# A four-layer gated block on one core: scores in quads of heads, gate weights spread on TensorE, gathers for depool and heads, another load queue, filler transposes, another order

## The reference

```python
x = x + tanh(g_xattn[0]) * L0_xattn(ctx, layernorm(x), mask, ...)   # cross attention, 8 heads of 16
x = x + tanh(g_ffn[0])   * L0_ffn(layernorm(x), ...)                # 4 of 16 attention heads of 64, picked per batch
x = x + tanh(g_xattn[1]) * L1_xattn(layernorm(x), ctx, lens, ...)   # depool of a scan over ctx, plus a projection
x = x + tanh(g_ffn[1])   * L1_ffn(layernorm(x), ...)                # 8 experts, top 2 per token, plus a shared one
```

## Time and profile before

| | before |
|---|---|
| runs | 243.16 us median of 3 (242.94 to 246.14) |
| profiled execution, first to last instruction | 242.8 us |
| PE busy | 211.0 us (87%), 1154 instructions |
| DVE busy | 151.1 us (62%), 464 instructions |
| ACT busy | 104.6 us (43%), 283 instructions |
| POOL busy | 54.0 us (22%), 95 instructions |
| mean granted TensorE clock | 0.895 |

### The profile page before, as it was taken

How to read it: one execution, slowest core, us unless ns; L and a number is a source line. 1 busy time by engine, 2 the same in 40 slices (tenths; PEclk the granted TensorE clock), 3 DMA queues, 4 the chain that set the end, 5 groups by cost and what they waited for, 6 DMA issues and landing times.

```text
span 242.8 us, 3827 instructions
## 1 busy us (share of the span) xinstructions
PE 211.0 (87%) x1154; PEld 152.9 (63%) x1154; DVE 151.1 (62%) x464; ACT 104.6 (43%) x283; POOL 54.0 (22%) x95
## 2 busy tenths in 40 slices
...
GB/s 198 293 82 195 79 230 327 1 65 54 33 44 72 65 45 25 3 1 0 1 37 33 0 0 37 34 0 3 22 0 0 4 1 22 0 3 0 0 0 43
DMA packets 17139, 12.45 MB, mean 51 GB/s; under 512 B 9024, under 2 KB 16416, under 8 KB 16992
## 3 DMA queue, kind: packets, MB, share of 16 engines
...
...
## 4 chain that ended last, share of the span: by engine, by line
PE 52%; DVE 1%; issue 1%; ACT 0%; ACTq 0%; DVEq 0%
PE dve_bank L655 7%; PE act_bank L647 7%; PE act_bank L648 6%; PE act_bank L650 4%; PE act_bank L594 3%; PE dve_bank L584 3%; PE act_bank L576 3%; PE dve_bank L640 2%; PE dve_bank L615 2%; PE dve_bank L669 2%; PE act_bank L660 2%; PE act_bank L449 2%; PE act_bank L561 1%; PE act_bank L512 1%; PE dve_bank L660 1%; PE dve_bank L612 1%
## 5 line engine op out<-in xcount | busy, mean ns | idle before, releaser
L769 ACT ACTIVATE hx<-act_bank,we 128x256 f32<-128x256 f32 x32 | 15.2, 475 | 36.1 <-PE act_bank L650 36.1
L1065 POOL TENSOR_TENSOR ctok<-ctok,cT 128x256 f32<-128x256 f32 x28 | 20.4, 729 | 44.6 <-DVE cT L994 43.5
L913 DVE TENSOR_REDUCE mx<-dve_bank 128x2 f32<-128x512 f32 x32 | 20.7, 686 | 10.4 <-PE dve_bank L496 10.3
L725 ACT ACTIVATE pT<-act_bank 128x512 f32<-128x512 f32 x32 | 17.6, 596 | 15.1 <-PE act_bank L512 14.9
L994 DVE SCALAR_TENSOR_TENSOR cT<-dve_bank,we,hx 128x256 f32<-128x256 f32 x32 | 15.0, 482 | 10.8 <-PE dve_bank L655 10.8
L1021 POOL TENSOR_SCALAR veps<-mv 128x2 f32<-128x2 f32 x16 | 3.1, 191 | 83.9 <-DVE mv L849 83.7
L647 PE MATMUL act_bank<-xw,we 128*128 128x256 f32 x64 | 20.3, 399 | 0.0
L655 PE MATMUL dve_bank<-hx,we 128*128 128x256 f32 x64 | 19.5, 404 | 0.2 <-ACT hx L770 0.2
L987 DVE TENSOR_TENSOR xw<-xnT,dve_bank 128x512 f32<-128x512 f32 x16 | 10.9, 684 | 13.3 <-PE dve_bank L640 13.3
L648 PE MATMUL act_bank<-xw,we 128*128 128x256 f32 x64 | 19.0, 379 | 0.0
L496 PE MATMUL dve_bank<-kstack,qstack 49*128 49x256 f32 x64 | 14.9, 368 | 4.5 <-DMA qstack<-parts 4.5
...
## 6 DMA issues: line engine op xcount, KB each, us to landing
we<-pack_e ACTq DMA_DIRECT2D x1, 1932.0 KB, 11.2
...
```

The lines of the kernel that those rows point to most:

```text
L725: act.activation(pT1[:, i].rearrange("p c t -> p (c t)"), bank[:], ACT.Exp, scale=HD1 ** -0.5).then_inc(act_done, 1)
L769: act.activation(hx[:, k % EXPERT_BUFS, 0, :], bank[:, 0:T], ACT.Silu, bias=X("b1")[:, i:i + 1])
L913: dve.tensor_reduce(mx[:, b, :, i], bank[:].rearrange("p (t s) -> p t s", t=TT), AX.X, ALU.max).then_inc(dve_done, 1)
L1065: ins = pool.tensor_tensor(yT[:, b % 2, :], yT[:, b % 2, :], prod[:, k % EXPERT_BUFS, :], ALU.add)
```

## The change

The program is rewritten in many places and its steps are put in another order. Part by part:

- **Scores.** A step of `s1` or `st1` now does four heads: each head stands in its own 32 partitions, with 16 rows of features, a row of the mask and a row of the maximum (17 or 18 contraction rows), as plain F32, and the four are issued to the four row groups in turn. There are two such steps a batch (`SETS`) for eight before. The projections give this layout themselves (twice the columns), so `parts` and all of `restack` are gone. The maxima come back through a transpose and a DVE addition into `qs` (`max1`), not a DMA. The mask is loaded as three rows and spread by a matmul (`masks`).
- **Heads.** `s2` takes two heads a step, issued to partitions 0 to 63 and 64 to 127 in turn. The bias of a head is one more column of its weights, and of the four loads SP issues two and POOL two, as indirect DMAs. `scale2` leaves DVE's 16 reciprocals and moves the 32 multiplications of 128x256 to POOL. Every second `pt2` is emptied by ACT instead of DVE.
- **Depool.** `plan_c` gives row numbers at once for all batches. DVE scales `dp`, SP stores it in DRAM, POOL gathers its rows with two indirect DMAs a batch (`gather`), and `base` adds them. The matmuls with `pick` are gone.
- **Experts.** `wide` does all four pairs in one step with F32 matmuls of 16 rows in four row groups. `b3` is a bias in ACT's copy, so L650 is gone; what it leaves out for the unchosen experts is taken from a small table (`ktab`) with one more matmul for each half of `y4`.
- **Loads.** Nearly all loads are issued from SP, at the start, in one sequence; ACT issues `pack_a`, the mask selectors and the second batch's `x`.
- **Fillers.** At 26 steps PE does 2 to 40 transposes of the identity into a bank that is taken next (180 in all), and 16 matmuls before the first step.
- **Rings.** Four banks each, for three and five.

```diff
-ACT_RING, DVE_RING = 3, 5
+ACT_RING, DVE_RING = 4, 4
...
+        "s1": (0, 4), "max1": (0, 1), "st1": (4, 0), "pv1": (1, 0), "heads1": (0, 1), "o1": (1, 0), "y1": (0, 1),
+        "route": (0, 1), "qkv2": (3, 0), "s2": (2, 0), "pv2": (1, 0), "y2": (0, 1),
...
+KEEP_WARM = {
+    ("norm", 1, 0): 8,
+    ("s1", 0, 1): 7,
...
+    ("norm", 1, 3): 40,
...
+            def keep_warm(step, count):
...
+                if n >= ring:
+                    pe.wait_ge(done, n - ring + 1)
+                for k in range(count):
+                    pe.transpose(bank[:, 0:P], ident, ident)
...
+                    banks = [take_dve(nd + j) for j in range(QUADS)]
+                    for t in range(TT):
+                        for j in range(QUADS):
+                            lo, hi = 32 * j, 32 * j + ROW_MAX
+                            mm = pe.matmul(banks[j][:, t * T:(t + 1) * T], qs[lo:hi, b % 2, i, t * P:(t + 1) * P],
+                                           ks[lo:hi, b % 2, i, :], start=True, stop=True, tile_position=(lo, 0))
...
-                    pe.matmul(bank[:, T:2 * T], X("w3")[:, i * D:(i + 1) * D], xe, start=True, stop=False
-                              ).then_inc(up_read, 1)
-                    pe.matmul(bank[:, T:2 * T], b3s[:, i, :], gT[:, b, :], start=False, stop=True
-                              ).then_inc(act_full, 1)
+                    pe.matmul(bank[:, T:2 * T], X("w3")[:, i * D:(i + 1) * D], xe, start=True, stop=True
+                              ).then_inc(act_full, 1)
...
-                    act.copy(hx[:, k % EXPERT_BUFS, 1, :], bank[:, T:2 * T]).then_inc(act_done, 1)
+                    act.activation(hx[:, k % EXPERT_BUFS, 1, :], bank[:, T:2 * T], ACT.Identity,
+                                   bias=X("b3")[:, i:i + 1]).then_inc(act_done, 1)
...
+                elif what == "scale2":
+                    pool.wait_ge(rec2_done, NA * b + i + 1)
+                    for t in range(TT):
+                        ins = pool.tensor_scalar(p2[:, b % 2, i, t, :], p2[:, b % 2, i, t, :], rec2[:, b, i, t:t + 1], 1.0,
+                                                 ALU.mult, ALU.mult)
+                    ins.then_inc(p2_scaled, 1)
...
+                elif what == "gather":
...
+                    pool.wait_ge(dp_out[b], 16)
+                    for t in range(TT):
+                        m = b * TT + t
+                        pool.indirect_dma_start(out=dpg[:, m, :], out_offset=None, in_=dp_rows[b],
+                                                in_offset=bass.IndirectOffsetOnAxis(ap=plug[:, m:m + 1], axis=0)
+                                                ).then_inc(dp_in[b], 16)
```

More of the change, by code:

```diff
@@ L68 @@
-ORDER = """
[L69 to L73, removed]
@@ new lines @@
+ORDER = """
+stat:0.0 masks:0.0 norm:0.0 stat:1.0 kv:0.0 q:0.0 masks:1.0 norm:1.0 s1:0.0 s1:0.1 max1:0.0 q:1.0 max1:0.1
+u:0.0 st1:0.0 kv:1.0 stat:2.0 st1:0.1 s1:1.0 pv1:0.0 pv1:0.1 gates:0.0 masks:2.0 heads1:0.0 s1:1.1 base:0.0
+o1:0.0 y1:0.0 max1:1.0 stat:0.1 ktab:0.0 masks:3.0 norm:0.1 norm:2.0 stat:3.0 max1:1.1 route:0.0 st1:1.0 q:2.0
+kv:2.0 st1:1.1 plan_a:0.0 s1:2.0 qkv2:0.0 pv1:1.0 s2:0.0 s2:0.1 scale2:0.0 depool:0.0 plan_b:0.0 scale2:0.1
+depool:1.0 max1:2.0 scale2:0.2 pt2:0.0 pv1:1.1 scale2:0.3 pt2:0.1 plan_c:0.0 pt2:0.2 heads1:1.0 pv2:0.0
@@ new lines @@
+base:0.1 pt2:0.3 gather:0.0 s1:2.1 pv2:0.1 o1:1.0 y2:0.0 st1:2.0 consts:0.0 base:0.2 base:1.0 stat:0.2
+max1:2.1 y1:1.0 stat:1.1 pv1:2.0 norm:0.2 norm:3.0 norm:1.1 y3:0.0 route:1.0 st1:2.1 q:3.0 gather:1.0 kv:3.0
+pv1:2.1 s1:3.0 qkv2:1.0 stat:0.3 depool:2.0 base:1.1 s2:1.0 heads1:2.0 scale2:1.0 s2:1.1 scale2:1.1 o1:2.0
+norm:0.3 scale2:1.2 pt2:1.0 pt2:1.1 scale2:1.3 max1:3.0 gather:2.0 pt2:1.2 gate:0.0 pt2:1.3 pv2:1.0 s1:3.1
+pv2:1.1 gate_t:0.0 y2:1.0 base:1.2 st1:3.0 max1:3.1 base:2.0 y1:2.0 st1:3.1 stat:2.1 stat:1.2 norm:2.1 pv1:3.0
@@ new lines @@
+norm:1.2 route:2.0 pv1:3.1 wide:0.0 shared:0.0 up:0.0 up:0.1 y3:1.0 stat:1.3 qkv2:2.0 up:0.2 s2:2.0 down:0.0
+heads1:3.0 down:0.1 s2:2.1 scale2:2.0 scale2:2.1 scale2:2.2 norm:1.3 scale2:2.3 pt2:2.0 pt2:2.1 pt2:2.2 o1:3.0
+pt2:2.3 gate:1.0 pv2:2.0 pv2:2.1 base:2.1 up:0.3 down:0.2 y2:2.0 up:0.4 base:2.2 base:3.0 stat:2.2 y1:3.0
+stat:3.1 down:0.3 shared:1.0 up:0.5 up:0.6 norm:3.1 norm:2.2 down:0.4 gate_t:1.0 route:3.0 up:0.7 wide:1.0
+down:0.5 up:1.0 down:0.6 y3:2.0 up:1.1 stat:2.3 down:0.7 qkv2:3.0 up:1.2 norm:2.3 s2:3.0 down:1.0 s2:3.1
@@ new lines @@
+y4:0.0 scale2:3.0 scale2:3.1 depool:3.0 down:1.1 scale2:3.2 gate:2.0 gather:3.0 down:1.2 pt2:3.0 shared:2.0
+scale2:3.3 up:1.3 pt2:3.1 up:1.4 pt2:3.2 up:1.5 down:1.3 base:3.1 gate_t:2.0 up:1.6 pt2:3.3 down:1.4 up:1.7
+wide:2.0 pv2:3.0 pv2:3.1 down:1.5 down:1.6 y2:3.0 stat:3.2 down:1.7 up:2.0 up:2.1 base:3.2 up:2.2 norm:3.2
+down:2.0 down:2.1 y3:3.0 up:2.3 stat:3.3 down:2.2 up:2.4 up:2.5 norm:3.3 down:2.3 gate:3.0 down:2.4 down:2.5
+y4:1.0 shared:3.0 gate_t:3.0 up:2.6 up:2.7 wide:3.0 up:3.0 down:2.6 up:3.1 down:2.7 up:3.2 down:3.0 down:3.1
@@ L121 @@
 NORMS = list(NORM_AT)
[L122 removed]
 XN_BUFS = 4
 EXPERT_BUFS = 3
+XW_BUFS = 4
+WARM_UP = 16
 def expert(k):
```

885 lines of the change are left out of this document (503 added, 382 removed), and 2 rows, old and new, of the table ROW_MAX.

## The result

The changed kernel takes 217.95 us (median of four executions, 214.15 to 219.52) against 243.18 before, a ratio of 0.884 with a 95% interval of 0.872 to 0.897: 11.6% faster. Each ratio here is taken from the executions in the faster of two states (here 214.15 and 216.92 us) and the kernel before run beside them, so it is not the quotient of the medians. The forecast was 202 us in a range of 186 to 224. So sign and range held, and the point lies 16 us too low. The profiled execution took 214.15 us, with a span of 212.4; against it the sum of 201.6 is 10.8 too low. The other executions differ from the profiled one in the granted clock (0.992 there, 0.966 to 0.984 in the others), and experiment 6 finds where.

What follows compares the result with a forecast made beforehand. Batch 0's chain with waits, partly at half clock, was taken to bound the time before the first wide matmul, PE's work the time behind it: 102.8 + 98.8 = 201.6, forecast 202 us, range 186 to 224.

Steps and rivals of the forecast that it cites:

- link 5: Batch 0's y2 to the first wide matmul: set by DVE's 30 us plus 3.5 for waits, 33.5 us.
- stage B: From batch 0's first wide matmul to the end: PE's work is the time, 112.3 - 18.2 + 4.7 = 98.8 us.
- rival (d): Fillers don't hold the clock before the first wide matmul, which stays at 1.2 GHz: slower, total 260 us; chance 0.05.
- Links 1 and 3: Batch 0: start to first scores, 20.6 to 14.0 us; y1 to first qkv2, 22.1 to 12.5 us.
- rival (e): Gathers fail their purpose, heads arrive no earlier, +5 in batch 0 and +5 behind: 212 us; 0.26 with (b), (c).
- Link 2: Batch 0's first scores to y1: less waiting for maxima and rs, cheaper pv1, kv of batch 1 added; 31.2 to 21.7 us.
- Link 4: Batch 0's first qkv2 to y2: POOL's scale2 at 2.6 us a head paces the softmax; 26.2 to 21.1 us.
- (b): Score matmuls on four row groups overlap only two at a time: +12, 214 us; chance 0.26 together with (c), (e).
- (c): POOL becomes the bound through scale2 and gathers, stalling down's three buffers: 217 us; chance 0.26 together with (b), (e).
- (a): POOL's scaling is cheap, 0.8 us a head, and waits overlap: 190 us; chance 0.22.
- stage A: Everything before the first wide matmul: batch 0's chain through three layers with waits and half clock; 130.5 to 102.8 us.

Runs made afterwards that it cites:

- experiment 6: Changed kernel with the ktab step moved later: 220.84 us; with ktab in place and 13 filler transposes added in and behind it: 216.1 us.
- experiment 3: Changed kernel with the scaling of the second softmax on DVE instead of POOL: 217.75 us.
- experiment 1: Changed kernel without its 180 filler transposes: 224.31 us; with only the 105 before the first wide matmul: 219.67; with only the 75 behind it: 221.91.
- experiment 5: Changed kernel with an added matmul of eight rows by 256 columns before the second matmul of every up, 32 in all: 244.5 us.
- Experiments 3 and 4: 3: changed kernel, softmax scaling on DVE, 217.75 us. 4: batch 0's first wide and shared moved earlier, eleven fillers out, 224.42; fourth up earlier, ten out, 218.46.
- experiment 2: Changed kernel with POOL's scaling of the second softmax in the one-operation form: 232.0 us; with only one column of 256 scaled: 216.3.

## Why the prediction was right, and where its size was off

**The waits were mis-sized; that is the main error.** In link 5 the prediction said that DVE sets the link, with 30 us, and allowed 3.5 for waits. DVE was busy 26.8, and more work on it does not lengthen the link (experiment 3). What fills it is PE's own work, 30.2, for which the prediction had 25.5 with all waits; that 30.2 is close to 30 is chance. The waits are 8.8: 5.3 more, the whole miss of that link. In stage B it reckoned 94.1 us of work for PE and 4.7 of waits; the work is 88.6 and the waits are 15.0. In the kernels without fillers the bare waits are 5.9 in link 5 (41.5 less 35.56) and 11.2 in stage B (104.6 less 93.4), so the two terms make 9 to 16 us too little.

The sentence that failed is the one that costed 75 fillers at nothing because PE must wait for batch 3's second layer. That something covers them is right (experiment 1: without them stage B is no shorter), but a wait that hides a filler takes time itself, and the sum still had the old 4.7. Nor is it that wait. Without fillers PE's longest one is for DVE's norm, in the second layer of batch 2 (the 3.68 us of experiment 1), and between the first `qkv2` and `y2` of batch 3 PE's timeline shows no wait.

Why the waits are so long can be read from PE's order. By the first matmuls, batch 1 takes 12.4 us from `y1` to `qkv2` and 16.3 from there to `y2` (70.58, 82.95, 99.27), batch 0 took 14.7 and 16.7, and the first `wide` stands behind all of it:

```profile
70.58 0.39 PE L581 MATMUL dve_bank<-wb,xnT 128*128 128x128 f32 x2
...
82.95 1.95 PE L598 MATMUL act_bank<-xnT,w2h 128*64 128x256 f32 x16
...
99.27 1.11 PE L641 MATMUL dve_bank<-wb,oT 128*128 128x128 f32 x8
...
108.83 1.15 PE L676 MATMUL dve_bank<-gT,wc 16*128 16x256 f32 x16
```

The prediction followed batch 0 link by link and the other batches mostly as load on DVE. PE's own work ahead of `wide` came to 85.7 us (100.9 busy less 15.2 of fillers, and 5.5 of it warm-up), where rival (d) reckoned 64. Experiments 3 and 4 fit this: more load on DVE did not lengthen the link, a later second layer of batch 2 lengthened the stage behind it.

**PE's work in stage B: right in kind, too small.** It fell by 19.0 us (107.6 to 88.6), or by 14.2 if the 93.4 of the kernel without stage B's fillers is taken (6.8 us of that stage were at half clock); 13.5 were reckoned. L650 was taken at 0.31; by the spacing in experiment 5 it cost 0.4 to 0.5, so 32 of them 13 to 16 us instead of 9.9.

**Links 1 and 3: as predicted,** +0.2 each, in the profiled execution. From picked heads to the first `qkv2` pass 6.7 us (44.8 to 51.5) and nothing on PE waits for the gathered weights; so rival (e), with its mark of 9, is out. That the loads set the link is not shown: PE's own work, most of it that of other batches, is 11.3 of its 12.7 us, and the sum had only the waits of batch 0, so the hit is in part luck. And link 3 holds only while the clock does, and that no step of the prediction looked at: 4 of the 16 us of the median (experiment 6).

**Link 2, +2.8.** The prediction added the `kv` of batch 1 that comes into this link, not its `q` and two of its scores, nor the 22 fillers (4.2 us of PE). Its DVE part is as told. No run takes these apart, so the share of each stays open.

**Link 4, -2.8.** The price of `scale2` was wrong: 0.97 us a head, not 2.6. The prediction had named 0.8 as the other end (15.1 for the link), and chose the 642 ns as the same operation; it was the same product in another form. Nor do the four heads, or the exponentials, pace the link, as the prediction had it: PE is busy 18.34 of 18.34 us, and with one column scaled the link stays as it was (experiment 2). The "GPSIMD Engine Reference" of the Trainium skill, section 4.1, from which the prediction estimated 1.4 us a head at most, was the nearer one, and the trace agrees with it for this form; in the form with one operation (1.84 a head) it does not. This error was lucky. Had POOL taken 920 ns, still less than the 1.28 assumed, the kernel would have stood at 232 us, 30 above the sum.

**The rivals.** (b) is out: quads cost 1.08. (c) is out: POOL is busy 40% of the span and 35% of link 4, and PE never waits for the buffers of `down`. (a) had the right price and the wrong result, as the waits did not shrink with it. (d) is out, and the trace speaks against the rule that made it. "TensorE: Matmul & The Clock Gate", Part 4, of the Trainium skill says that the full clock "doesn't engage for transpose-mode". The fillers are transposes, and forty of them in a wait kept it at 1.00 where it fell to 0.50 without them (experiment 1).

What no run takes back one by one is the rest of stage A: quads of scores, the loads' new queue, the gathers. Their share of its 21.7 us is read from the marks of the links and not tested.
